# Attention block on one core: two tiles of cross attention taken together on TensorE, self attention pieces placed behind each tile's scores

## What is computed

```python
x = x + xattn(layernorm(x), ctx, ctx)   # 16 heads of width 8, 2048 context rows
x = x + attn(layernorm(x))              # 16 heads, rotary q and k, bias by distance
x = x + ffn(layernorm(x))               # 16 experts of 512, softmax over the best 4
```

## Time and profile before

| | |
|---|---|
| median of 3 runs (lowest to highest) | 209.88 us (209.35 to 210.08) |
| the profiled execution: its time | 209.72 us |
| its span, first to last instruction | 207.8 us |
| TensorE matmul busy | 190.0 us (91%) |
| VectorE busy | 144.4 us (69%) |
| ScalarE busy | 143.9 us (69%) |
| GpSimd busy | 82.4 us (40%) |
| granted TensorE clock, mean | 0.998 of full |

### The profile page before, as it was taken

One profiled execution on the slowest core, in us unless ns is written; L12 is line 12 of the kernel. 1 busy time (PEld: TensorE's weight loads), 2 busy tenths in 40 slices (PEclk: granted clock), 3 DMA queues, 4 the chain that ended last, 5 costly groups with the idle time before them and its releaser, 6 DMA issues.

```text
span 207.8 us, 6327 instructions
## 1 busy us (share of the span) xinstructions
PE 190.0 (91%) x2552; PEld 134.1 (65%) x2552; DVE 144.4 (69%) x259; ACT 143.9 (69%) x321; POOL 82.4 (40%) x117
## 2 busy tenths in 40 slices
PE   4799988999999989989999999999879999999991
PEld 1335235656666545655655666897759998999981
DVE  5289998797979978989999945856884438222220
ACT  4768766888897978876797976778574545456660
POOL 6222979997786987110201001510000005078400
PEclk9999999999999999999999999999999999999999
DMA  5834333366334732367868701400000000000000
GB/s 122 295 140 183 145 93 93 99 221 226 93 93 105 203 106 78 98 209 214 278 222 250 244 19 24 185 0 0 5 0 0 3 0 13 3 0 5 0 0 21
DMA packets 8688, 21.24 MB, mean 102 GB/s; under 512 B 1664, under 2 KB 2784, under 8 KB 8656
## 3 DMA queue, kind: packets, MB, share of 16 engines
q1 hardware_dynamic: 7344, 19.47, 29.3%
q0 software_dynamic: 592, 0.74, 1.6%
q10 hardware_dynamic: 720, 0.59, 0.9%
HBM read 17.52 MB, written 3.28 MB: 100 GB/s over the span
## 4 chain that ended last, share of the span: by engine, by line
PE 61%; DVE 15%; POOL 7%; DMA 6%; issue 4%; ACT 3%; SPq 2%; ACTq 1%; DVEq 0%
PE ps L1516 13%; PE ps L1266 11%; PE ps L1549 10%; PE ps L1247 8%; PE ps L1212 5%; PE ps L1122 3%; DMA wks<-in_wk 3%; DVE sm L712 2%; PE ps L1116 2%; SPq L327 2%; DMA parts_d<-w1s 2%; POOL wr L505 1%; DVE kst L710 1%; DMA kst<-parts_d 1%; PE ps L1409 1%
## 5 line engine op out<-in xcount | busy, mean ns | idle before, releaser
L609 DVE TENSOR_REDUCE mx<-ps 128x2 f32<-128x1024 f32 x64 | 75.2, 1221 | 7.6 <-PE ps L1212 7.5
L1025 ACT ACTIVATE ex<-ps 128x512 f32<-128x512 f32 x128 | 69.4, 594 | 15.0 <-PE ps L1247 12.1
L1266 PE MATMUL ps<-ex,vau 128*9 128x128 f32 x1024 | 39.9, 274 | 0.5 <-ACT oS L1040 0.4
L1516 PE MATMUL ps<-xT,w1s 128*128 128x128 f32 x256 | 34.4, 278 | 0.2
L1516 PEld LDWEIGHTS ps<-xT,w1s 128*128 128x128 f32 x256 | 31.1, 192 | 1.7 <-ACT cT L1051 0.8
L1247 PE MATMUL ps<-qst,kst 64*128 64x128 bf16 x512 | 30.2, 217 | 1.5 <-ACT ex L1025 1.1
L807 DVE SCALAR_TENSOR_TENSOR xs<-ps,wr,xs 128x128 f32<-128x128 f32 x32 | 11.2, 350 | 28.6 <-PE ps L1549 28.3
L1266 PEld LDWEIGHTS ps<-ex,vau 128*9 128x9 f32 x1024 | 22.0, 90 | 13.7 <-ACT ex L1025 9.7
L1247 PEld LDWEIGHTS ps<-qst,kst 64*128 64x128 bf16 x512 | 18.5, 94 | 16.9 <-ACT ex L1025 9.1
L1212 PE MATMUL ps<-kst,qst 64*128 64x512 bf16 x128 | 27.2, 382 | 1.7 <-DMA kst<-parts_d 0.8
L1051 ACT ACTIVATE cT<-ps,b1s 128x128 f32<-128x128 f32 x64 | 18.2, 370 | 13.8 <-PE ps L1516 13.8
(11 more groups left out here) (205 smaller groups left out, 250.4 us busy)
## 6 DMA issues: line engine op xcount, KB each, us to landing
kst<-parts_d SPq DMA_DIRECT2D x84, 64.0 KB
w1s<-in_w SPq DMA_DIRECT2D x8, 512.0 KB, 4.2
kst<-in_w SPq DMA_DIRECT2D x8, 512.0 KB, 4.5
parts_d<-w1s SPq DMA_DIRECT2D x4, 768.0 KB, 3.8
cT<-in_ctxT SPq DMA_DIRECT2D x3, 512.0 KB, 5.0
cT<-in_ctxT SPq DMA_DIRECT2D x2, 256.0 KB, 5.0
picks<-in_pick ACTq DMA_DIRECT2D x1, 384.0 KB, 5.4
qkvs<-in_qkvw POOLq DMA_DIRECT2D x1, 192.0 KB, 3.6
```

The lines of the kernel that those rows point to most:

```text
L609: dve.tensor_reduce(out=mx2[:, b, 2 * pair:2 * pair + 2, f], in_=ps[:, bank:bank + 2, :], axis=AX.X, op=ALU.max).then_inc(s["redA"], 1)
L1025: act.activation(ex[:, e % NE, :], ps[:, EBANK["exp", e], :], ACT.Exp, scale=SCALE).then_inc(s["exp"], 1)
L1266: last = pe.matmul(ps[32 * j:32 * j + DK + 1, 7, 128 * hg:128 * hg + 128], vau[:, NK * b + c, GH * hg + j, :], ex[:, (2 * t + j % 2) % NE, ...
L1516: last = pe.matmul(ps[:, SELF[j % 2], 128 * n:128 * n + 128], w1s[:, f0:f0 + 128], xT[:, (b % B) * S:(b % B + 1) * S], start=True, stop=True)
```

## The change

Tiles are taken in twos. `paired(t)` holds for all tiles with a unit to come except 32 and 33 (where bank 7 changes from batch 0 to batch 1). A pair with a job now has unit, job, unit between the scores of its tiles; a pair without one splits the second tile's scores around its unit. The values of both tiles before the next pair's scores stand in one run. From tile 52 on there are pairs too, with both self attention pieces ahead of the values. Jobs move to even tiles. `ex` has six slots, of which the last two first hold `picks` and `qr`; ScalarE therefore waits for `qsq` ahead of the loop.

```diff
-        picks = sb("picks", [128, 2, 2, 3, 128], bf16)
-        qr = sb("qr", [128, B * S])
-        NE = 4
+        NE = 6
+        early = ex[:, 4:NE, :].rearrange("p a k -> p (a k)")
+        picks = early[:, 0:768].bitcast(bf16).rearrange("p (q h t m) -> p q h t m", q=2, h=2, t=3)
+        qr = early[:, 768:768 + B * S]
...
-        SMALL_AT = {34: "sums", 36: "heads", 39: "proj", 41: "normed", 43: "qkv", 47: "qkT"}
-        VALS_AT = {3: 5, 11: 6, 19: 7}
+        SMALL_AT = {34: "sums", 36: "heads", 40: "proj", 42: "normed", 44: "qkv", 48: "qkT"}
+        VALS_AT = {4: 5, 12: 6, 20: 7}
...
+        def paired(t):
+            return t // 2 != TILES // 4 and t + 8 + LEAD < N_UNITS
...
-                if u == 51:
+                if u == 52:
                     normed(1, [0])
...
-                if t >= 2:
-                    act.wait_ge(s["pv"], t - 1)
+                if t >= NE // 2:
+                    act.wait_ge(s["pv"], t - NE // 2 + 1)
...
             v_piece(4, V_BANK[4])
+            act.wait_ge(s["qsq"], 1)
...
-            for t in range(TILES):
-                if ring_job(t - 1):
-                    scores(t, (0,))
-                    next_unit(t)
-                    scores(t, (1,))
-                else:
-                    scores(t)
...
-                if not ring_job(t - 1):
-                    next_unit(t)
-                self_first(t)
+            def two_tiles(t):
+                scores(t)
+                next_unit(t)
+                if ring_job(t):
+                    job(t)
+                    next_unit(t + 1)
+                    scores(t + 1)
+                else:
+                    scores(t + 1, (0,))
+                    next_unit(t + 1)
+                    scores(t + 1, (1,))
                 if t:
                     values(t - 1)
+                values(t)
+
+            def one_tile(t):
+                scores(t)
+                job(t)
+                next_unit(t)
+                self_first(t)
+                values(t - 1)
+
+            def two_last(t):
+                scores(t)
+                job(t)
+                self_first(t)
+                scores(t + 1)
+                self_first(t + 1)
+                values(t - 1)
+                values(t)
+
+            for t in range(0, TILES, 2):
+                if paired(t):
+                    two_tiles(t)
+                elif t > TILES // 2:
+                    two_last(t)
+                else:
+                    one_tile(t)
+                    one_tile(t + 1)
```

More of the change, by code:

```diff
@@ L456, in _ @@
             pool.wait_ge(s["qparts"], 1)
-            link(pool.tensor_tensor(qf[:], qr[:], qp[:, 0, :], ALU.add))
+            link(pool.tensor_tensor(qf[:], qr, qp[:, 0, :], ALU.add))
             pool.tensor_tensor(qsq[:], qf[:], qf[:], ALU.mult).then_inc(s["qsq"], 1)
@@ L580, in q_parts @@
                 dve.wait_ge(s["q0"], 1)
-                link(dve.scalar_tensor_tensor(out=qr[:], in0=ps[:, 7, B * S:2 * B * S], scalar=cols[:, 0:1], in1=qp[:, 0, :],
+                link(dve.scalar_tensor_tensor(out=qr, in0=ps[:, 7, B * S:2 * B * S], scalar=cols[:, 0:1], in1=qp[:, 0, :],
                                               op0=ALU.add, op1=ALU.subtract))
-                link(dve.tensor_copy(qp[:, 1, :], qr[:]))
-                dve.tensor_tensor(qp[:, 2, :], qr[:], qp[:, 1, :], ALU.subtract).then_inc(s["qparts"], 1)
+                link(dve.tensor_copy(qp[:, 1, :], qr))
+                dve.tensor_tensor(qp[:, 2, :], qr, qp[:, 1, :], ALU.subtract).then_inc(s["qparts"], 1)
             def norms_max(bank):
@@ L930, in _ @@
             act.dma_start(wqs[:], wq).then_inc(d_wq, 16)
-            act.dma_start(picks[:].rearrange("p q h t m -> p (q h t m)").bitcast(i32), pick_in).then_inc(d_pick, 16)
+            act.dma_start(early[:, 0:768].bitcast(i32), pick_in).then_inc(d_pick, 16)
             act.wait_ge(s["pool"], 1)
@@ L1481, in next_unit, with job @@
                     unit(t + 8 + LEAD)
-            for t in range(TILES):
-                if ring_job(t - 1):
-                    scores(t, (0,))
-                    next_unit(t)
-                    scores(t, (1,))
-                else:
-                    scores(t)
+            def job(t):
                 if turns(t):
```

## The result

The changed kernel takes **211.02 us** (median of 7 runs, 210.66 to 211.34) beside 209.36 us for the kernel before (7 runs, 209.18 to 210.08): ratio 1.0072, with a 95% interval of 1.0054 to 1.0090. It is slower by about 0.7%. The forecast was 209.8 us and no change that can be measured. The time lies inside the range, but nearer to the second rival, slow release (211.4 us), than to the forecast.

The account below looks back on a forecast made before the run. No engine was full; VectorE, TensorE and bank loops lay close, with the bank loop to hold plain pairs and VectorE tiles 34 to 51. -0.7 - 0.9 + 1.2 + 0.3 = -0.1 gave 209.8 us, range 208.3 to 211.5.

Parts of the forecast that it names:

- second rival, slow release: Banks come back 0.13 after an exponential, not 0.05, lengthening every pair outside VectorE's stretch: 211.4 us; chance 0.25.
- loop through the bank: Plain pairs: half scores wait for the first exponential to free their bank, giving 2.38 to 2.39 us against 2.32.
- first rival, VectorE's pace: Half scores do not wait out the exponential; plain pairs take 2.27 to 2.3 us, whole 208.2 us; chance 0.31.
- rival that the turn still waits: Units 23 and 31 not reduced earlier, so GpSimd stays at 76.14 and 1.6 us gain vanishes: 211.4 at most; chance 0.06.
- 0.42 + 0.49 + 0.59 + 0.05 = 1.55: Pairs with a turn: second scores wait for the first tile's second exponential plus 0.05 release; pair 2.88 us against 2.85.
- -0.7: Tiles 0 to 29: first pair, 8 plain, 3 turn and 3 V pairs, 39.4 us against 40.1.
- Tiles 30 and 31: Unit 31 is reduced earlier, so the turn no longer waits for GpSimd: 2.88 us instead of 3.76, -0.9.
- Tiles 34 to 51, +1.2: VectorE's work 24.65 + 0.5 plus 2.5 idle at four small-step waits: 27.6 us against 26.4.
- Here VectorE decides: Tiles 34 to 51: VectorE, busy 24.65 of 26.39 us, sets the pace and waits for jobs now behind a unit.
- The last stretch, +0.3: Tile 52 to the projection: savings outweighed by 2.5 us of new waits for exponentials, 18.0 to 18.1 us against 17.75.
- of which I count 1.1 as waits: Tile 52 to the projection: 1.1 of the earlier 17.75 us counted as waits and taken off, 0.35 and 0.51 the large ones.
- five joined runs save 5 x 0.12: Tile 52 to the projection: five joined values runs save 0.6 us in all.

Follow-up runs that it names:

- halves_apart: Changed kernel with second scores asked for in two successive halves, in pairs with a non-V job and from tile 52 on: 210.44 us, ratio 1.0048.
- last_pairs: Kernel before, with pairs only in tiles 52 to 63 and six exponential slots: 210.68 us, ratio 1.0047.

## Why the prediction was wrong

**What held.** Joined values take 1.00; plain pairs are 2.40 (2.38 to 2.39 forecast), held by the loop through the bank; V pairs 3.17 (3.19); no wait for GpSimd at tile 30, group 4 ready at 74.35 (74.1); VectorE's waits 0.89, 0.88, 0.42, 0.35 (1.0, 0.75, 0.45, 0.3), 2.54 in all (2.5); in the last stretch the waits at 54, 60 and 62 are 0.94, 0.44 and 0.52 (0.9, 0.65, 0.5). The first rival, VectorE's pace, fell: a plain pair did not go below 2.38 until the exponential itself was shortened. What the Trainium skill says in "TensorEngine Tiling (Array Packing)", Tiling Modes, Key Properties, of the drain at a change of mode agrees with the trace: two values runs cost 1.00 instead of 1.12. It did not set the time: in plain pairs the saved 0.12 went into the wait for the bank. The rival that the turn still waits did not come true either.

**What failed.** The steps are the release of the banks, sized at 0.05 for whole scores where it was 0.12, and the self attention stretch, where five joins and the waits taken away were counted too high. By stretch the forecast is off by 0.54, 0.13, 0.38 and 0.52, all on the same side:

1. *The release, in "0.42 + 0.49 + 0.59 + 0.05 = 1.55"* for pairs with a turn. Whole scores load 0.12 behind the exponential and run 0.15 behind it (T = 1.66), so a turn pair is 2.98, not 2.88: 0.3 in tiles 0 to 29. The prediction gave 0.05 "since what ran before is a unit of the same form". In the changed kernel a unit of the same form ran before and the release was still 0.12. What tells the two prices apart is whether whole or half scores wait: `halves_apart` had 0.05 in the same place. With the first two pairs (2.20 and 2.47 against 2.13 and 2.38), 0.02 more on each plain pair and 0.02 less on each V pair this makes the 0.54 between -0.7 and -0.16. It is the second rival's mechanism, but not its size: that rival put 0.08 on plain pairs as well. That its 211.4 came near the 211.02 is in part luck: it asked 1.6 us of the release, and `halves_apart` got 0.8 back with the short one.
2. *Tiles 30 and 31*: the same 0.11 (2.99 for 2.88).
3. *Tiles 34 to 51, +1.2*: the idle time was sized right where it is a wait (2.54 of 2.5), and VectorE's busy time too (25.16 for 25.15). The other 0.27 of its 2.81 idle are gaps that the walk did not count; with 0.04 in the waits and the rounding this makes +1.58 of +1.2. But a sum of busy and idle time comes out whatever holds the pace. "Here VectorE decides" held only in part: the pairs at 34, 36, 40 and 48 stand at 2.97 to 2.99, the length that their own exponentials give them, and `halves_apart` took 0.21 off the stretch.
4. *The last stretch, +0.3.* The term was 17.75 - 1.1 - 0.6 - 0.56 + 2.5. The new waits are 2.60, so their sum was near, with 0.70 at 56 where 0.45 stood and less at 60. At 56 the prediction had tile 56's exponentials 0.42 behind their scores and did not see what ScalarE must do first: its self attention exponential at 115.80 waited 0.45 for VectorE, and tile 56's exponentials stand behind it, 0.97 behind their scores (115.37 to 116.34). The 0.61 that VectorE waited at its first self attention step is not the cause: in `last_pairs` that wait is gone and the 0.70 stays. The larger miss is in what was taken off: without its waits the stretch is 18.57 - 2.60 = 15.97, not 15.49. Half of this 0.48 is "of which I count 1.1 as waits": the rows show 0.35 and 0.51, 0.86 in all, and the rest is gaps of 0.03 to 0.06 of which it is not shown that the change takes them away. The other half is "five joined runs save 5 x 0.12": the pairs at 52, 54 and 56 saved some 0.1 each; those at 58 and 60 saved nothing. Pair 58 takes 3.38 as before, with no wait in either kernel. TensorE in tile 58, the change first and the kernel before second:

```profile
119.51 0.41 PE L1414 MATMUL ps<-cT,v2s 128*9 128x128 f32 x8
119.85 0.40 PE L1252 MATMUL ps<-qst,kst 64*128 64x128 bf16 x8
```

```profile
118.75 0.41 PE L1409 MATMUL ps<-cT,v2s 128*9 128x128 f32 x8
118.98 0.62 PE L1266 MATMUL ps<-ex,vau 128*9 128x128 f32 x16
```

The product with V has the same form as the values and was joined to them already. Behind it values come after 0.23, scores after 0.34. The change makes one join and undoes another, which the prediction did not count.

The costs that the prediction set at nothing: the new wait on `qsq` shows as a first exponential 0.48 behind the first scores (34.44 to 34.92) where it was 0.42. That is 0.06, once. That the wait is the cause was not tried.

What the prediction missed as a whole is the sign inside the sum. It saw -1.6 and +1.5 side by side and took the total as the answer. The runs show that the parts come apart: up to tile 33 the change gains (0.9961 alone), from 34 on it loses, and within the gaining part the plain and turn pairs lose as well.

Left open: why whole scores take 0.07 longer to start than half scores behind such an event, and how the +1.58 of tiles 34 to 51 divides between VectorE's waits and the pairs' own length.

## What to carry to other kernels

In this kernel, joining runs of one form on an engine paid only where that engine held the loop. With three banks in turn, whole scores followed each other no closer than 1.16 to 1.17 us while the exponential took its 0.59, and 0.12 us saved on TensorE became a wait; the pairs paid only around the V jobs, where TensorE's own work, 3.17 us, holds the pair. When a change applies one form to a whole loop, price each kind of iteration apart and keep the form where it wins: here pairs at the three V jobs alone gave 207.6 us, and pairs nearly everywhere 211.0. Ready work put into a wait did not help where the waiting instruction starts the next turn of the loop: the turn pairs kept 2.92 of their 2.98.

## What the chip showed that was not expected

- The start of a matmul run behind the same ScalarE event depends on what waits: 0.05 us to the weight loads for four matmuls on one half of the rows, 0.12 for eight on both, whether the array had stood 0.2 us or 1.
- A single plain tile, too, was on the bank loop (0.42 + 0.59 + 0.15 = 1.16 us) and not on VectorE's 1.13 or TensorE's 1.10: with an exponential shorter by 0.105 it fell to 1.10.
- V jobs as pairs shortened single turn tiles that were not touched: 2.70 us where they took 2.85. The turn stands 0.34 behind the scores (42.96 - 42.62) instead of 0.49, since its bank comes from the second exponential of tile 5. In the kernel before that is the fourth of six exponentials without a gap (the run starts at 40.98 and takes 3.42), done at about 43.27, and the turn's loads start at 43.35; here it is done at 41.73 + 1.08 = 42.81, earlier than the turn needs it. The six slots are not the cause: `last_pairs` has them too, with V jobs at single tiles, and its turn tiles take 2.85 with the turn at 0.48.
